# Layer-0 row maxima: split and turned ahead of the next group's first maximum, and two of the four transfers into the rows of q issued by ScalarE's queue

## The reference, cut to what matters

```python
q = q.reshape(bs, seq, N_HEADS, HEAD_DIM).transpose(0, 2, 1, 3)
attn = jnp.einsum('bhqd,bkd->bhqk', q, k) / math.sqrt(HEAD_DIM)
attn = jnp.where(causal[None, None], attn, jnp.float32(-1000000000.0))
attn = jax.nn.softmax(attn, axis=-1)
out = jnp.einsum('bhqk,bkd->bhqd', attn, v)
```

## Time and profile before

| what | us |
|---|---|
| median of 3 runs | 1310.63 (1310.13 to 1314.87) |
| the profiled execution, its own time | 1310.77 |
| its span, first to last instruction | 1309.0 |
| mean granted TensorE clock | 0.971 of full |
| busy: TensorE, VectorE, ScalarE, GpSimd | 1192.1, 935.0, 686.7, 681.0 |
| DMA, mean over the span | 60 GB/s |

### The profile page before, as it was taken

How to read it: one execution, slowest core, us unless ns; L and a number is a source line. 1 busy time by engine, 2 the same in 40 slices (tenths; PEclk the granted TensorE clock), 3 DMA queues, 4 the chain that set the end, 5 groups by cost and what they waited for, 6 DMA issues and landing times.

```text
span 1309.0 us, 22523 instructions
## 1 busy us (share of the span) xinstructions
PE 1192.1 (91%) x6940; PEld 870.5 (67%) x6940; DVE 935.0 (71%) x2757; ACT 686.7 (52%) x1599; POOL 681.0 (52%) x679
## 2 busy tenths in 40 slices
PE   6888897988569999999999999999999999999998
PEld 5445464545447677686786777867767777667787
DVE  5767787775567786877867868778778687676553
ACT  3356646564354645546546455465465564654432
POOL 0340101011135799998579999857999999000000
PEclk9789999999779999999999999999999999999999
DMA  6431012000124210320420302132022000000000
GB/s 219 132 80 50 26 50 89 26 34 1 65 85 125 76 38 0 135 70 30 139 95 5 129 7 70 49 121 92 26 111 69 2 33 32 0 2 1 17 17 33
DMA packets 36102, 77.93 MB, mean 60 GB/s; under 512 B 8152, under 2 KB 22336, under 8 KB 35248
## 3 DMA queue, kind: packets, MB, share of 16 engines
q1 hardware_dynamic: 26736, 47.13, 10.8%
q0 software_dynamic: 8128, 25.49, 6.0%
q10 hardware_dynamic: 1152, 4.19, 0.8%
HBM read 54.62 MB, written 22.04 MB: 59 GB/s over the span
## 4 chain that ended last, share of the span: by engine, by line
PE 37%; DVE 25%; issue 8%; ACT 3%; DVEq 0%; ACTq 0%
PE bank L1494 10%; PE bank L1468 7%; DVE qk L1093 6%; DVE qkst L1069 5%; PE bank L1479 5%; PE bank L297 5%; PE bank L299 5%; PE bank L298 5%; DVE negmax L1164 2%; DVE probs L1159 2%; DVE x L1149 2%; DVE ytmps L1146 1%; DVE sm L131 1%; DVE sm L129 1%; PE bank L1455 1%
## 5 line engine op out<-in xcount | busy, mean ns | idle before, releaser
L711 POOL TENSOR_SCALAR gtmp<-gidx,lut 128x344 f32<-128x344 int32 (+2 forms) x210 | 299.5, 1426 | 21.3
L1468 PE MATMUL bank<-kT,qT 128*128 128x128 f32 (+3 forms) x512 | 181.7, 444 | 13.2 <-ACT probs L887 13.1
L714 POOL TENSOR_TENSOR gacc<-gacc,gtmp 128x344 f32<-128x344 f32 (+2 forms) x210 | 183.6, 874 | 17.5
L887 ACT ACTIVATE probs<-bank,negmax 128x128 f32<-128x128 f32 (+3 forms) x256 | 135.1, 528 | 60.6 <-DVE negmax L1164 57.0
L297 PE MATMUL bank<-wgH,hL 128*128 128x512 f32 x384 | 155.3, 404 | 1.1 <-issue 1.1
L1164 DVE TENSOR_REDUCE negmax<-bank 128x1 f32<-128x128 f32 (+3 forms) x256 | 122.6, 483 | 42.4 <-PE bank L1469 40.5
L298 PE MATMUL bank<-wgL,hH 128*128 128x512 f32 x384 | 152.3, 397 | 0.0
L299 PE MATMUL bank<-wgH,hH 128*128 128x512 f32 x384 | 152.1, 396 | 0.0
L1494 PE MATMUL bank<-pT,v 128*128 128x512 f32 (+3 forms) x512 | 149.2, 434 | 0.8 <-ACT pT L879 0.7
L1103 DVE TENSOR_REDUCE negmax<-bank 128x1 f32<-128x512 f32 (+3 forms) x176 | 108.1, 636 | 57.4 <-PE bank L1398 57.0
L1069 DVE BATCH_NORM_STATS2 qkst<-qk 128x6 f32<-128x128 f32 x512 | 109.4, 280 | 46.4 <-issue 46.4
(11 more groups left out here) (221 smaller groups left out, 2682.4 us busy)
## 6 DMA issues: line engine op xcount, KB each, us to landing
hH<-h_saved SPq DMA_DIRECT2D x16, 512.0 KB, 4.0
hL<-h_saved SPq DMA_DIRECT2D x16, 512.0 KB, 4.9
qst<-q_parts SPq DMA_DIRECT2D x96, 64.0 KB, 2.4
w_saved<-shi POOLq DMA_DIRECT2D x24, 256.0 KB, 2.3
w_saved<-slo POOLq DMA_DIRECT2D x24, 256.0 KB, 2.6
sraw<-in_wqkv POOLq DMA_DIRECT2D x18, 256.0 KB, 3.0
wgH<-w_saved SPq DMA_DIRECT2D x3, 1536.0 KB, 8.4
wgL<-w_saved SPq DMA_DIRECT2D x3, 1536.0 KB, 11.6
```

Source lines behind the costliest of these rows:

```text
L711: link(pool.tensor_scalar(tmp if j else acc, part, float(j), lut1[0:rows, j:j + 1], ALU.is_equal, ALU.mult))
L714: link(pool.tensor_tensor(acc, acc, tmp, ALU.add))
L1468: pe.matmul(bank[SCORE_BANKS[i % 3]][:, 0:n], qT[:, h, t * P:n], kT[:, h, 0:n], start=True, stop=False)
```

## The change

The block that splits and turns a group's maxima stands ahead of the maximum of the same step in VectorE's program. SP issues the transfers j = 0 and 1; ScalarE issues j = 2 and 3, in the step of the turn, behind the exponential and ahead of its other pieces, after a wait for `nm_turned`. Counts on `nm_ready` stay.

```diff
+        def negmax_rows(g):
+            return qst[SHIFT:ROWS0, g * HG * SEQ:(g + 1) * HG * SEQ].rearrange("p (i j q) -> p i j q", j=QT, q=VW)
...
                 sp.wait_ge(nm_turned, b * NG + g + 1)
-                rows = qst[SHIFT:ROWS0, g * HG * SEQ:(g + 1) * HG * SEQ].rearrange("p (i j q) -> p i j q", j=QT, q=VW)
-                for j in range(QT):
-                    sp.dma_start(rows[:, :, j, :], nmt[j * VW:(j + 1) * VW, :]).then_inc(nm_ready, 16)
+                for j in range(QT // 2):
+                    sp.dma_start(negmax_rows(g)[:, :, j, :], nmt[j * VW:(j + 1) * VW, :]).then_inc(nm_ready, 16)
...
                                    ACT.Exp).then_inc(exp0, 1)
+                for i, b in at(s, GU, SLOTS0):
+                    if i % GU == 0:
+                        g = i // GU
+                        act.wait_ge(nm_turned, b * NG + g + 1)
+                        for j in range(QT // 2, QT):
+                            act.dma_start(negmax_rows(g)[:, :, j, :], nmt[j * VW:(j + 1) * VW, :]).then_inc(nm_ready, 16)
                 for i, b in at(s, VALUE + 1, SLOTS0):
...
             for s in range(-1, (NB - 1) * SLOTS0 + AFTER + CHAIN):
+                for i, b in at(s, GU, SLOTS0):
+                    if i % GU == 0:
+
+                        g = i // GU
+                        nm = negmax[:, g * ITEMS:(g + 1) * ITEMS]
+                        dve.wait_ge(max0, b * SLOTS0 + (g + 1) * GU)
+                        ch_nm.step(dve.tensor_copy(nmp[:, 0, :], nm))
+                        ch_nm.step(dve.tensor_tensor(nmp[:, 1, :], nm, nmp[:, 0, :], ALU.subtract))
+                        if b * NG + g:
+                            dve.wait_ge(nm_ready, (b * NG + g) * QT * 16)
+                        dve.transpose(nmt[:, :], nmp[:, :, :].rearrange("p j i -> p (j i)")).then_inc(nm_turned, 1)
                 for i, b in at(s, 0, SLOTS0):
...
                                       AX.X, ALU.max, negate=True).then_inc(max0, 1)
-                for i, b in at(s, GU, SLOTS0):
-                    if i % GU == 0:
...
-                        dve.transpose(nmt[:, :], nmp[:, :, :].rearrange("p j i -> p (j i)")).then_inc(nm_turned, 1)
                 for i, b in at(s, VALUE + 2, SLOTS0):
```

More of the change, by code:

```diff
@@ L1096, in _ @@
             for s in range(-1, (NB - 1) * SLOTS0 + AFTER + CHAIN):
[L1097 to L1105, removed]
                 for i, b in at(s, GU, SLOTS0):
@@ L1116, in _ @@
                         dve.transpose(nmt[:, :], nmp[:, :, :].rearrange("p j i -> p (j i)")).then_inc(nm_turned, 1)
+                for i, b in at(s, 0, SLOTS0):
+                    g, (j, h, heads) = i // GU, UNITS[i % GU]
+                    t = QT - 1 - j
+                    w = (t + 1) * P
+                    to = g * ITEMS + h * QT + t
+                    dve.wait_ge(s0_pe, b * SLOTS0 + i + 1)
+                    dve.tensor_reduce(negmax[:, to:to + (heads - 1) * QT + 1:QT],
+                                      bank[S_BANKS[(b * SLOTS0 + i) % 3]][:, 0:heads * w].rearrange("p (h k) -> p h k", h=heads),
+                                      AX.X, ALU.max, negate=True).then_inc(max0, 1)
                 for i, b in at(s, VALUE + 2, SLOTS0):
```

## The result

The changed kernel is slower: 1336.9 us median of 4 runs (1331.3 to 1342.4) against 1310.9 before, a ratio of 1.019 with a 95% interval of 1.014 to 1.025. The forecast was 1316.6 with a range up to 1322. The direction of the likeliest case was right, its size was not: +26 us for +5.8.

What follows compares the result with a forecast made beforehand. TensorE was taken to bound the kernel, waiting for the rows of maxima. Group effects of -3.4, +8.2, +1.0 and +1.4 gave +7.2; 1.4 taken back left +5.8 on 1310.8, so 1316.6 us, range 1302 to 1322.

Steps and rivals of the forecast that it cites:

- the likeliest case: Whole change: slower by 5.8 us, to 1316.6 us; chance 0.45, its own range 1312 to 1321.
- the prize: TensorE's waits for the rows of maxima at a group's first transposed score: 17.9 us, 1.4% of the time.
- Part 1: Two of four transfers on ScalarE's queue: rows land 1.29 us sooner; two issues cost ScalarE 1.27 us.
- the twins: Same-shaped 512 KB load on SP (0.320 us) and store on ScalarE (0.326), read as the queue not mattering.
- Part 2: VectorE's turn ahead of the maximum: cast 0.6 us earlier, maximum ends 0.6 us later, VectorE's work unchanged.
- Part 3: ScalarE's new wait for the turn, delaying later exponentials; group 11's score u+3 1.78 us late.
- the sum: All 16 groups: -3.4 +8.2 +1.0 +1.4 = +7.2, less 1.4 taken back, leaving +5.8 us.
- A: Faster: the hold falls into ScalarE's idle room everywhere, gaining 10.5 us, 1300.3; chance 0.18.
- B: Nothing: an issue on ScalarE costs 0.33 to 0.45 us, gains and holds cancel, 1308 to 1311; chance 0.18.
- C: Slower by more: VectorE further behind, ScalarE's wait for the turn grows in the stalled groups; +10, 1321; chance 0.17.
- the seven stalled groups: Groups 1, 2, 4, 5, 6, 9, 13, where TensorE waited for the rows: together -3.4 us.
- D: Change fails its aim: ScalarE arrives late and its two transfers land last; chance 0.02.

Runs made afterwards that it cites:

- filled pair: Six repeats of a score product per group but the first, added to the changed kernel (1326.8 us) and to the kernel with the early turn only (1310.0 us).
- run 24: Not a follow-up run: "run" is a verb here, TensorE had just executed 24 products of 16 columns without a gap.

## Why the prediction was wrong, point by point

**What bounds the kernel, and the prize.** Right. TensorE bounds the stage, and the rows of maxima were the wait to remove: the early turn alone takes 11.4 of its 17.9 us away and 7.6 off the time.

**Part 1, the price of an issue on ScalarE.** Right in kind: the twins on two queues pointed to SP's 0.611, measured 0.646. Low in sum: I took 1.27 us for two, the pairs take 1.28 to 1.46, and 2.18 in group 0.

**Part 2, the early turn.** Its gain is real and its danger small, as said. That it is worth 7.6 us by itself stood in no sum, since each group was worked out only with ScalarE's part in it.

**Part 3, the holds.** Right as far as they go. For group 11 I had a turn, two issues and a late exponential, in the order in which the changed kernel shows them:

```profile
243.39 1.46 ACTq L850 DMA_DIRECT2D qst<-nmt  x2
244.90 0.98 ACT L842 ACTIVATE pT<-bank 128x384 f32<-128x384 f32 x2 [2.13 <-issue]
...
243.15 0.21 DVE L1115 STREAM_TRANSPOSE nmt<-nmp 128x32 bf16<-128x32 bf16 x1
...
245.44 0.43 PE L1386 MATMUL bank<-qst,kst 98*128 98x512 bf16 x1 [1.72 <-ACT pT L842]
...
250.57 0.64 PE L1386 MATMUL bank<-qst,kst 98*128 98x512 bf16 x1
254.38 0.64 PE L1386 MATMUL bank<-qst,kst 98*128 98x512 bf16 x1
```

TensorE stood 1.72 us there (the forecast had it 1.78 late). But from that product to the group's first transposed score it took 254.38-245.44 = 8.94 us, where the earlier trace rows have 236.44-231.60 = 4.84, for the same instructions. The durations say why: 0.64 us for the product, at the lower clock. In group 0 VectorE's L959 (now L967) waited 2.37 us for khi and started at 61.51; the forecast had 59.9, with 1.27 us for the issues that took 2.18 and the end of the turn at 57.95, where it came at 58.57. In total TensorE's idle time grew by 2.6 us, where the sum had it 5.8 us late. One slip of the sum changes nothing: its upper end comes to 5.8+1.0+1.4 = 8.2, not 8.4.

**The step that failed** is the sum itself: it worked each group "from its own timeline", late starts with the durations of before, took 5.8 us from it as the whole change, and ended with "What I have not counted is a change of TensorE's granted clock". That term was 26.2 us, ten times the growth of idle time. The forecast left the clock at what it was before, 0.95 in this stage, without a reason. I named the term and gave it neither a price nor a place in the range, though the rows to bound it were there. The same product takes 0.39 us at the higher level and 0.61 at the lower one, in group 0 of the kernel before:

```profile
62.56 0.61 PE L1378 MATMUL bank<-qst,kst 98*128 98x512 bf16 x1 [2.18 <-DMA qst<-nmt]
```

**The rivals.** A (room on ScalarE) is refuted: 1.24 us of copies there cost 18.9 us. B (an issue at 0.33 us) is refuted by 0.646. C (slower by more) had the right sign, but its mechanism, a longer wait for the turn, is refuted: the wait alone costs 2.6 us, and its place, the seven stalled groups, lost 4.8 of the 33.6. D is refuted: TensorE no longer waits for the rows at all.

What stays open: why the second transfer on ScalarE costs 23.0 us and the first 8.0. The clock of the profiled executions (0.90 and 0.84) goes the same way, but no run here varies the length of a hold in finer steps. Open too is which waits bring the clock down. The sum of the idle times does not tell, nor does their length: the kernel before has nine of 1.5 us or more in the stage (the longest 2.53) and 27 us at the lower level, the changed one eleven (the longest 2.94) and 89 us. The filled pair shows that work in the holds keeps the clock up, not what the clock answers to in each one.

## What to carry to other kernels

Before moving a DMA's issue to a compute engine's queue, look at what that engine feeds: two issues of 0.65 us ahead of its next result are a hold of 1.3 to 1.5 us each time, whatever its busy share says. Where TensorE bounds a stage and has short waits, price every new wait twice, once as idle time and once at the durations of the lower clock over the work behind it, and put the second into the range. Measure the halves of a change alone: here one half was worth -7.6 us and the other +33.6.

## What the runs showed of the hardware that was not expected

TensorE's clock fell in this stage with no single idle time over 2.94 us. Of the ten idle times of 1.7 to 2.6 us in the changed kernel behind group 0, six have a fall of the clock within 2 us of their end (at 163.7, 211.5, 245.7, 269.6, 303.7 and 320.8 us), and four have none (they end at 99.3, 147.2, 230.0 and 236.2). In the stretch at the lower level TensorE can be busy all the time (13.00 of 13 us from 164 us on). Two falls have no idle time of more than 0.3 us in the five us ahead: at 116.0, and at 187.6, where TensorE had just run 24 products of 16 columns without a gap (columns as in the table of stretches):

```profile
187.48 0.26 PE L297 MATMUL bank<-w0H,wft 128*128 128x16 f32 x1
...
185.20:187.60 2.40, 2.40 (x24) 2.38 (x22) 2.33 (x11) 0.00 (x0) 0.00 (x0) 1.00 0.00 0
187.60:197.90 10.30, 8.95 (x37) 4.30 (x37) 7.26 (x17) 3.74 (x8) 0.00 (x0) 0.50 0.01 1
```

The Trainium skill ("TensorE: Matmul & The Clock Gate", A second HAM failure mode: psum-queue depth-cycling) describes a kernel that goes through its banks in turn, where frequent short idle times between groups of matmuls make the clock swing between its two levels. This case's trace agrees in that the clock swings here too, nine times down in the stage; that short idle times are the whole reason it does not bear out, since two of the falls have none.

Across the runs the stage's clock does not follow TensorE's idle time: 39.8 us of it went with 0.84, and 51.1 us, of which 27.4 in one stall, with 0.89. In that run the clock was low once from 57 to 94 us, the stall included, and for 20 us in the rest of the stage. And adding 90 useless matmuls made the kernel faster by 10.1 us.

An issue on ScalarE's queue starts beside a running exponential: in group 14 of the changed kernel both begin at 300.2, the exponential for 0.49 us and the issues for 1.36. So one of two bounds of the forecast, that issuing waits for the exponential's end, is excluded there.
